# A graph network's last layer: the first six adjacency blocks are asked for during the node math before it

## The reference

```python
x = _layernorm(x + _L2_gnn_ref(x, edge_index, W_l, W_r, att, bias))   # attention over edges, softmax by target node
x = _layernorm(x + _L3_gnn_ref(x, edge_index, W1, b1, W2, b2))

def _gcn_layer(x, row, col, W, b):
    agg = jax.ops.segment_sum(x[col], row, num_segments=N)
    deg = jnp.clip(jax.ops.segment_sum(ones, row), 1.0, None)[:, None]
    return (agg / deg + x) @ W + b
h = jax.nn.relu(_gcn_layer(x, row, col, W1, b1))
h = _gcn_layer(h, row, col, W2, b2)
```

## Time and profile before

| | |
|---|---|
| median of 3 runs | 4365.61 us |
| lowest, highest | 4355.29, 4366.24 us |
| the profiled execution's own time | 4373.95 us |
| its span, first to last instruction | 4372.3 us |
| mean granted TensorE clock | 0.613 of full speed |
| busy share PE, DVE, ACT, POOL | 51%, 51%, 15%, 59% |

### The profile page before, as it was taken

The page is one execution under the profiler, slowest core; times in us unless marked ns, Lnnn a source line. Parts: engine busy times, 40 slices in busy tenths (PEclk is TensorE's granted clock), DMA queues, the critical chain, the costliest instruction groups (busy, mean ns, idle before and its releaser), DMA issues. The chain is left out here.

```text
span 4372.3 us, 79196 instructions
## 1 busy us (share of the span) xinstructions
PE 2241.3 (51%) x19380; PEld 1689.7 (39%) x19381; DVE 2245.4 (51%) x4750; ACT 666.9 (15%) x1478; POOL 2579.3 (59%) x2627
## 2 busy tenths in 40 slices
PE   3343333333325542555555555436666666664997
PEld 1333333233324432444444444324444444442332
DVE  5532111121137745666666666647777777777001
ACT  0011111111124410111111111101111111111000
POOL 0477777777742215777777777137777777772000
PEclk8555555555555555666666666556666766765999
DMA  1453334343346645666666666135555555553954
GB/s 38 149 136 128 126 124 131 116 135 122 107 115 193 194 48 145 171 171 166 171 169 171 170 170 170 29 75 153 154 152 155 155 150 158 155 151 80 337 183 145
DMA packets 641999, 630.49 MB, mean 144 GB/s; under 512 B 127546, under 2 KB 472794, under 8 KB 641856
## 3 DMA queue, kind: packets, MB, share of 16 engines
q1 hardware_dynamic: 356958, 357.61, 27.4%
q0 software_dynamic: 89104, 141.91, 13.9%
q10 hardware_dynamic: 195858, 130.02, 9.8%
HBM read 444.40 MB, written 186.44 MB: 144 GB/s over the span
## 5 line engine op out<-in xcount | busy, mean ns | idle before, releaser
L1537 POOL DMA_INDIRECT rows<-nodes_xl,id_slot x832 | 821.1, 987 | 394.6 <-issue 248.9
L1537 POOL DMA_INDIRECT rows<-nodes_kv,id_slot x832 | 831.1, 999 | 319.8 <-issue 248.3
L826 POOL DMA_INDIRECT msg_by_src<-message,place_slot x832 | 833.1, 1001 | 264.3 <-issue 253.1
L779 PE MATMUL picked<-X,hotT 128*128 x1664 | 373.2, 423 | 636.3 <-issue 361.7
L779 PEld LDWEIGHTS picked<-X,hotT 128*128 128x128 f32 x1664 | 360.2, 331 | 650.6 <-issue 650.6
L1936 PE MATMUL sums<-parts,hot 128*128 128x68 bf16 (+1 forms) x4992 | 325.6, 251 | 383.9 <-DVE parts L1717 383.9
L1733 DVE SCALAR_TENSOR_TENSOR running_counts<-running_counts,same_block,counts_p 128x128 f32<-128x128 f32 x1040 | 357.5, 344 | 278.6 <-PE counts_p L1892 170.0
L734 DVE TENSOR_TENSOR message<-picked,w_dst 128x512 f32<-128x512 f32 x104 | 71.9, 691 | 790.6 <-ACT message L799 756.4
L1936 PEld LDWEIGHTS sums<-parts,hot 128*128 128x128 bf16 x4992 | 312.1, 167 | 405.4 <-issue 405.4
L1892 PE MATMUL counts_p<-hot_src,hot_blocks 128*128 128x128 bf16 x2080 | 247.3, 277 | 222.4 <-DVE running_counts L1733 220.8
L1892 PEld LDWEIGHTS counts_p<-hot_src,hot_blocks 128*128 128x128 bf16 x2080 | 196.0, 155 | 259.4 <-DVE running_counts L1733 233.1
(11 more groups left out here) (402 smaller groups left out, 3656.4 us busy)
## 6 DMA issues: line engine op xcount, KB each, us to landing
hot_src<-hot_src_by_cell SPq DMA_DIRECT2D x1040, 64.0 KB
adjacency<-running_counts ACTq DMA_DIRECT2D x1040, 64.0 KB
loc_all<-loc_by_cell SPq DMA_DIRECT2D x104, 512.0 KB
hotT<-hotT_by_step SPq DMA_DIRECT2D x208, 256.0 KB
hot<-hot_by_step SPq DMA_DIRECT2D x208, 256.0 KB
blocks<-adjacency SPq DMA_DIRECT2D x40, 1280.0 KB
hot_by_step<-hot ACTq DMA_DIRECT2D x104, 256.0 KB, 2.0
hotT_by_step<-hotT ACTq DMA_DIRECT2D x104, 256.0 KB, 2.2
```

Of the source, the lines that this page charges most:

```text
L779: ins = nc.tensor.matmul(picked[:, s, 2 * q + g, :], hotT[:, s, 2 * q + g, :], X[:, bass.ds(n, 1), :].rearrange("p a c -> p (a c)"), start ...
L826: pool.indirect_dma_start(out=msg_dram, out_offset=bass.IndirectOffsetOnAxis(ap=ids[:, s, t:t + 1], axis=0), in_=rows[:, s, t, :], in_offs ...
L1537: pool.indirect_dma_start(out=rows[:, j, t, :], out_offset=None, in_=table, in_offset=bass.IndirectOffsetOnAxis(ap=ids[:, j, t:t + 1], axis=0)
```

## The change

Six units (`AHEAD`) are issued in another Block: `node_math` gets a hook `meanwhile` that gives SyncE code, and `node_math(layer2)` uses it to issue units 0 to 5. `last_layer` issues the others. For that `blocks` is allocated before `layer2`, so the tensors that only the attention loop needs (`near`, `product`) are now given back together before it; `rest` has no tensor of its own and is put where `xl` was, a view with 66 words from one node tile to the next of which 64 are used; the ten semaphores of the slots are made before the second attention layer, in an ExitStack of their own (`late`), which is closed before the store.

```diff
+AHEAD = 6
...
-        def group_loads(eng, blocks, loaded, used, units, held):
+        def group_loads(eng, blocks, loaded, used, units, held, upto=None):
-            for f, (g, d) in enumerate(units[held:]):
+            for f, (g, d) in enumerate(units[held:upto]):
...
-                u = slot_of(units, at, held)
+                u = at % SLOTS if units[0] == (0, 0) else slot_of(units, at, held)
...
-        def last_layer(blocks):
+        units = [(g, d) for g in range(len(SRC_GROUPS)) for d in range(NT // DSTS)]
+        def last_layer(blocks, loaded, rest):
...
-                rest = sbuf("rest", [P, NT, D], ctx=c)
...
-                    loaded = [sem(f"loaded{u}", c1) for u in range(SLOTS)]
...
-                        group_loads(sp, blocks, loaded, used, units, 0)
+                        group_loads(sp, blocks, loaded, used, units, AHEAD)
...
-        def node_math(body, norms=1):
+        def node_math(body, norms=1, meanwhile=None):
...
+                @block.sync
+                def _(sp):
+                    if meanwhile is not None:
+                        meanwhile(sp)
...
+        late = ExitStack()
+        blocks_in = [sem(f"blocks_in{u}", late) for u in range(SLOTS)]
         with ExitStack() as c:
-            near = sbuf("xr_parts", [P, 3, 4 * 512], BF16, ctx=c)
             xl = sbuf("xl", [P, NT, D + 2], ctx=c)
...
+            c2 = ExitStack()
+            near = sbuf("xr_parts", [P, 3, 4 * 512], BF16, ctx=c2)
...
             c2.close()
+            blocks = sbuf("blocks", [P, SLOTS, 4, DSTS, P], ctx=c)
...
-            node_math(layer2)
-        with ExitStack() as c:
-            blocks = sbuf("blocks", [P, SLOTS, 4, DSTS, P], ctx=c)
-            last_layer(blocks)
+            node_math(layer2, meanwhile=lambda sp: group_loads(sp, blocks, blocks_in, None, units, 0, AHEAD))
+            last_layer(blocks, blocks_in, xl[:, :, 0:D])
+        late.close()
```

More of the change, by code:

```diff
@@ L1180, in slot_of @@
             return (len(units) - 1 - at % SLOTS) % SLOTS
-        def last_layer(blocks):
-            units = [(g, d) for g in range(len(SRC_GROUPS)) for d in range(NT // DSTS)]
+        units = [(g, d) for g in range(len(SRC_GROUPS)) for d in range(NT // DSTS)]
+        def last_layer(blocks, loaded, rest):
             back = units[::-1]
@@ L1310, in _ @@
                         dve.wait_ge(kept, len(SRC_GROUPS))
-                        step(nc.vector.tensor_tensor(rest[:], Y[:], X[:], ALU.add))
-                        step(nc.vector.tensor_tensor(rest[:], rest[:], rowwise(b2_s[:]), ALU.add))
+                        step(nc.vector.tensor_tensor(rest, Y[:], X[:], ALU.add))
+                        step(nc.vector.tensor_tensor(rest, rest, rowwise(b2_s[:]), ALU.add))
                 with ExitStack() as c1, nc.Block() as block:
@@ L1372, in last3 @@
                 def last3(step, sq, a, b):
-                    step(nc.vector.tensor_tensor(X[:], X[:], rest[:], ALU.add))
+                    step(nc.vector.tensor_tensor(X[:], X[:], rest, ALU.add))
                     layernorm(step, X, sq, a, b)
@@ L2229, in gnn @@
                 store([(node_view("xl"), xl[:])])
-            c2 = ExitStack()
             product = sbuf("score_a", [P, TB, D], ctx=c2)
```

## The result

Timed side by side, 20 runs each, the changed kernel has a median of 4360.63 us (4349.5 to 4368.13) and the kernel before 4368.68 us (4355.29 to 4380.07): a ratio of 0.9983, 95% interval 0.9975 to 0.9991. That is 8.05 us less, 0.18%, under the 0.3% that was taken as the bound of "the same", though the interval lies clear of 1: by it the gain is between 4 and 11 us, so the times alone can't tell 8.05 from 5 or 10. The profiled execution's span is 4357.0 us for 4372.3, 15.3 less; only part of that is the change, as follows.

What follows compares the result with a forecast made beforehand. It took the tail as one chain with a single hole, PE waiting 8.69 us for bytes. -8.69 + 0 + 0.44 = -8.25 us off the 4365.61 median gave 4357.4 us, own range 4356 to 4359, 8 in 10 within 4345 to 4368.

Steps and rivals of the forecast that it cites:

- The hole: Between PE's transposes and first matmul on a unit: the wait for bytes disappears, -8.69 us.
- The first `mean_T`: Sign in the last layer: VectorE's operation behind the first five units starts at about 4062.4 for 4071.15.
- The issues: SyncE's six early issues in layer2's Block take at most 12.1 us, covered by its 21.2 us wait.
- a rival at 0.08: Layer2's Block: late loads or held SyncE lose part of the gain, time about 4363 us; chance 0.08.
- The other transfers: Bias, degrees and later units in the last layer: no second wait; degrees have 14 us of slack.
- The clock: PE's half-clock stretch at the first units: 0, kept within -0.5 to +0.8 us.
- The barrier: Extra semaphore clearing and barrier between last layer norm and store: +0.44 us, between 0 and 0.88.
- `rest` in `xl`'s place: Three VectorE operations on rows 66 words apart keep their pace: 0.
- VectorE beside the bytes: Layer2's node math slowed by arriving units; at twice the length the time is 4378 us; chance 0.03.
- The instruction fetch: At the new Block, code fetched beside a full DMA delays entry, at most 8.7 us; within the 0.08 rival.
- The attention loop: New `xr_parts` address makes its matmuls 5% faster or slower, 6.3 us: 4351 or 4364; chances 0.06 and 0.04.

Runs made afterwards that it cites:

- ahead0: The changed kernel with no unit issued ahead (0 for 6): tail 358.96 us, 0.9997 of the kernel before.
- ahead1: The changed kernel with one unit issued ahead for six: PE waits 3.12 us for blocks, tail 353.25 us.
- deg_third: The kernel before with the row of degrees issued behind the first two units: wait 5.16 us, tail 356.02 us.
- ahead10: The changed kernel with ten units issued ahead for six: no wait for blocks, tail 351.10 us.
- after_again: The changed kernel unaltered, run in a later set of rounds: tail 351.08 us, 0.999 of the kernel before.
- no_late: The changed kernel with the ten slot semaphores given back in the first pass's clearing, without the extra end barrier: tail 348.62 us, 0.9986 of the kernel before.
- ahead2: The changed kernel with two units issued ahead for six: no wait for blocks, tail 350.53 us.

## Why the prediction was right

*The hole*: -8.69 us reckoned, -8.76 in the timeline, and back with 8.97 when the issues are put back (`ahead0`). That it was bytes in a queue and not a start-up cost is what `ahead1` and `deg_third` show, each by a wait of another length at the place that was reckoned. The first `mean_T` was foretold for 4062.4 on the clock of the trace before; it started at 4055.42, and with the 6.97 us by which this tail began earlier that is 4062.39.

*The issues*: the bound was 12.1 us for six, with the first unit there 8.8 us behind its issue; they took 8.89, and SyncE still waited 12.1 us for VectorE. The bound was wide because that unit was read behind the row of degrees. That the queue holds the issuing engine, and that this becomes the Block's end when there are too many, was a rival at 0.08 with its point at 20.7 us; `ahead10` passes that point and pays 1.4 us.

*The other transfers*: the degrees arrived 6.6 us behind their issue (ScalarE's copy at 4037.98), before 6.1, and `mean_T` wanted them at 4055.42: the slack held.

*The clock*: taken as 0 within -0.5 to +0.8. In the profiled pair it was 0, and that was luck. Over the tails but `ahead1`'s, the 50 instructions of the first five units took from 22.66 to 24.37 us, so -0.7 to +1.0 about the 23.33, and the start of the second pass, for which the prediction had no term, moves too (24.23 to 25.74 us in its first 70). The second profile of the changed kernel (`after_again`) lost 0.92 and 0.46 us there: its tail of 351.08 is a gain of 6.97 us, just outside the bounds of -9.2 to -7.0. The term was right in its middle and too narrow in its bounds.

*The barrier*: +0.44 reckoned, +0.45 measured, and gone again with `no_late`.

*`rest` in `xl`'s place*: the two sums take 1.82 us each, and so does the last operation that reads it, as before.

*VectorE beside the bytes*: its operations take 1.82 to 1.83 us with the DMA engines at 390 GB/s, where they took 1.82 to 1.83 with none. That rival is out. The Trainium skill ("SBUF — State Buffer", Who interferes with whom) says that a DMA never contends with a compute engine, and these rows agree.

*The instruction fetch*: PE entered the new Block 2.76 us behind VectorE's last start in both kernels (4028.27 to 4031.03, and 4035.23 to 4037.99). From 4009 to 4033 of the changed kernel only SyncE's queue moved packets (3312 of them, 7.87 MB), so no code was fetched beside the units, and nothing waited for it.

*The attention loop*: the matmuls that read `xr_parts` took 221 ns in the changed kernel for 220, so the address cost next to nothing. But the start of the tail lies between 4006.85 and 4015.90 us in four kernels of one layout and one loop code (changed, `ahead0`, `ahead1`, `ahead10`). That is 9 us from execution to execution, as large as the change, so the 6.97 us that the profiled pair shows ahead of the tail need no cause in it; and `ahead0`, with the new addresses, was timed as the kernel before within 0.12%.

The sum of -8.25 us met -8.33 in the tail and -8.05 in the medians. The mechanism is shown; that both figures lie within 0.2 us of the sum is luck in part, since the same kernel's second tail gave -6.97 and its second set of rounds -6.4. The forecast time, 4357.4, is 3.2 us under the 4360.63, and 3.1 of that is the start: the median of before, 4365.61 then from 3 runs, was 4368.68 from 20.

## What to carry to other kernels

Look for stretches of the timeline in which one engine alone works and then the DMA engines alone: at a border between Blocks both are one hole, and its price is the wait in the row of the waits, no more. Closed in part it can give less: `deg_third` took 3.5 us off the wait and 2.0 (again, 2.9) off the tail. Move as many transfers as the consumer needs to live on until the next ones land (two here; the other four bought nothing), and not so many that the issuing engine is held past the end of the work that covers it. For a few us in some thousands, read the stretch from a fixed point near the change to the end in each profile: it answers to 1 us or a little more where the whole time, with loops that vary by 9 us, needs tens of runs.

## What the runs showed of the hardware that I had not expected

- TensorE's granted clock stayed at 0.50 of full (1.2 of 2.4 GHz) for very different lengths behind the same rest of 29 us and four transposes. Where the units follow at once, it lasted 3.3 us into the units in the changed kernel, 5.2 in the same kernel run again, 4.4 in `ahead2` and 2.0 in `no_late`; behind a wait, 3.3 in the kernel before and 5.5 in `deg_third`. In `ahead1` it stood at 1.00 all through a wait of 3.1 us and fell 0.5 us after the matmuls came back.
- On chips 12 and 4 the loops took some 1440 us more than in the first set of rounds, with the tail unchanged. In the lines of `ahead2` VectorE waits 1198.8 us ahead of `running_counts` for what the view calls "remote"; in the kernel before that group's idle time was 278.6 us in all. Its instructions themselves take 345 ns for 344.

```profile
L1732 DVE SCALAR_TENSOR_TENSOR running_counts<-running_counts,same_block,counts_p 128x128 f32<-128x128 f32 x1040 | 358.7, 345 | 1409.3 <-remote 1198.8 <-PE counts_p L1891 107.8 <-issue 35.1
```

That operation waits for its slot of `runs` to be stored to the adjacency in HBM, so slower stores are what I would suspect. No run separated it, nor the chip from the time at which it was used, and the cause stays open.
